# All expert weights resident on the chip; VectorE copies a tile's first half, TensorE streams the second from a register address

## The reference

```
p = softmax(LN(x) @ gate_w); pick the 2 best of E = 8 experts per token
h = gelu(LN(x) @ w1[e] + b1[e])        # w1[e]: 128 x 512
y = h @ w2[e] + b2[e]                  # w2[e]: 512 x 128
out = x + LN(x) ... + sum over the 2 experts of p_e * y_e
```

## Time and profile before

| | |
|---|---|
| profiled execution | 472.98 us; its span, first to last instruction, 471.3 us |
| granted TensorE clock, mean | 0.947 of 2.4 GHz |
| busy: TensorE, weight loads, VectorE, ScalarE, GpSimd | 397.6, 311.8, 280.9, 213.8, 137.6 us |
| DMA | 53.72 MB, mean 114 GB/s |
| weights by tile, `w1s` and `w2s` | 42 DMAs each, 256 KB, 3.5 us to landing |
| chain that ended last | PE 36%, issue 22%, DVE 18%, POOL 9%, DMA 6%, SyncE's queue 4% |

### The profile page before, as it was taken

One profiled execution on the slowest core, in us unless ns is written; L12 is line 12 of the kernel. 1 busy time (PEld: TensorE's weight loads), 2 busy tenths in 40 slices (PEclk: granted clock), 3 DMA queues, 4 the chain that ended last, 5 costly groups with the idle time before them and its releaser, 6 DMA issues.

```text
span 471.3 us, 8956 instructions
## 1 busy us (share of the span) xinstructions
PE 397.6 (84%) x2864; PEld 311.8 (66%) x2864; DVE 280.9 (60%) x905; ACT 213.8 (45%) x456; POOL 137.6 (29%) x139
## 2 busy tenths in 40 slices
PE   3547959989999999999999975979898898867963
PEld 2335747574488655885578634869798787866863
DVE  1388798799998689878987699323611011012322
ACT  1229376717636436322632351355543455534421
POOL 7743051431301250021642366010300000064343
PEclk9986979999999999999999995998979899999988
DMA  5999200000000000000400012424655778897542
GB/s 153 351 376 428 113 0 2 3 0 1 1 1 1 2 1 1 1 2 1 156 24 1 11 36 73 140 58 130 198 182 183 237 235 269 248 302 231 185 153 67
DMA packets 36117, 53.72 MB, mean 114 GB/s; under 512 B 5722, under 2 KB 20065, under 8 KB 34793
## 3 DMA queue, kind: packets, MB, share of 16 engines
q1 hardware_dynamic: 33512, 47.66, 30.1%
q0 software_dynamic: 2560, 5.52, 3.9%
HBM read 40.18 MB, written 12.98 MB: 113 GB/s over the span
## 4 chain that ended last, share of the span: by engine, by line
PE 36%; issue 22%; DVE 18%; POOL 9%; DMA 6%; SPq 4%; ACT 4%; POOLq 0%; DVEq 0%; ACTq 0%
POOL qkv L743 4%; PE bank L882 3%; PE bank L935 3%; DMA qkv<-experts_out,arena 3%; PE bank L948 3%; PE bank L964 3%; PE bank L987 2%; PE bank L920 2%; POOL dealt L729 2%; PE bank L980 2%; PE bank L972 2%; DVE h L1729 2%; PE bank L929 2%; SPq L567 2%; SPq L568 2%
## 5 line engine op out<-in xcount | busy, mean ns | idle before, releaser
L1275 ACT ACTIVATE arena<-bank,arena 128x128 f32<-128x128 f32 x168 | 47.9, 371 | 62.8 <-PE bank L1062 62.2
L743 POOL DMA_INDIRECT qkv<-experts_out,arena x28 | 26.5, 946 | 98.7 <-issue 80.2
L1070 PE MATMUL bank<-w2s,arena 128*128 128x128 f32 x336 | 48.0, 290 | 1.3 <-ACT arena L1275 1.3
L1070 PEld LDWEIGHTS bank<-w2s,arena 128*128 128x128 f32 x336 | 44.4, 205 | 2.3 <-ACT arena L1275 1.1
L729 POOL DMA_INDIRECT dealt<-xy,arena x28 | 32.5, 1161 | 29.2 <-DVE arena L1662 21.5
L1717 DVE COPY big<-bank 128x128 f32<-128x128 f32 x22 | 6.3, 290 | 46.6 <-PE bank L1070 46.6
L1062 PE MATMUL bank<-big,w1s 128*128 128x128 f32 x176 | 24.1, 281 | 10.2 <-DMA w1s<-in_ew 7.1
L1062 PEld LDWEIGHTS bank<-big,w1s 128*128 128x128 f32 x176 | 21.3, 191 | 12.5 <-issue 6.5
L1062 PE MATMUL bank<-arena,w1s 128*128 128x128 f32 x160 | 24.1, 299 | 5.9 <-DMA w1s<-in_ew 5.9
L935 PE MATMUL bank<-xT_f,wq 128*128 128x512 f32 x64 | 28.9, 597 | 0.0
L1062 PEld LDWEIGHTS bank<-arena,w1s 128*128 128x128 f32 x160 | 21.8, 211 | 7.3 <-issue 4.9
(11 more groups left out here) (266 smaller groups left out, 959.2 us busy)
## 6 DMA issues: line engine op xcount, KB each, us to landing
w1s<-in_ew SPq DMA_DIRECT2D x42, 256.0 KB, 3.5
w2s<-in_ew SPq DMA_DIRECT2D x42, 256.0 KB, 3.5
dealt<-lb SPq DMA_DIRECT2D x7, 1024.0 KB, 13.3
big<-in_tv SPq DMA_DIRECT2D x2, 2048.0 KB
big<-in_ew SPq DMA_DIRECT2D x16, 256.0 KB, 4.6
big<-dealt SPq DMA_DIRECT2D x22, 64.0 KB, 2.0
arena<-dealt SPq DMA_DIRECT2D x20, 64.0 KB, 1.8
experts_out<-arena SPq DMA_DIRECT2D x5, 256.0 KB, 4.1
```

The source lines that it names most:

```text
L743: pool.indirect_dma_start(yg[:, k, t, :], None, ys[g], bass.IndirectOffsetOnAxis(ap=posi[g][:, k, at:at + 1], axis=0)).then_inc(s_yg[b], 16)
L1070: last = pe.matmul(p[:, 0:D], hid[n % 2][:, c * P:(c + 1) * P], w2s[n % WAYS][:, c * D:(c + 1) * D], start=(c == 0), stop=(c == FC - 1))
L1275: last = act.activation(hid[n % 2][:, c * P:(c + 1) * P], of("K.up", n)[:, c * P:(c + 1) * P], ACT.Gelu, bias=eb1[:].rearrange("p e c -> p ...
```

## The change

All 8 experts' weights become resident in `big` (`rw1`, `rw2`, 4 MB, the whole buffer). V0 to V7 load them, at the head of SyncE's list. Section L is gone. Instead VectorE gets a phase K.0: a register load of `eid`, then a copy of 128x512 from `big` at a register address into `w1s` (still a ring of three). K.3 on TensorE gets a register load of `eid`, and its moving operand is read from `big` at a register address. K.1 is as before but waits for the copy. J reads `rw1`, `rw2` in place. What lay in `big` moves: tiles from 20 on into the buffers `u`, `fs`, `sq` of layer 0, J's hidden tiles into `ht`. All five lists are reordered.

```diff
     "K.dve2": ["y"],
+    "K.dve": ["w1"],
...
-        w1s = [sb("w1s%d" % i, [P, FF]) for i in range(3)]
-        w2s = [sb("w2s%d" % i, [P, FF]) for i in range(3)]
+        w1s = [sb("w1s%d" % i, [P, FF]) for i in range(WAYS)]
...
+        rw1 = big[:, 0:E * FF].rearrange("p (e f) -> p e f", e=E)
+        rw2 = big[:, E * FF:].rearrange("p (e f) -> p e f", e=E)
+        rest = [x[:].rearrange("p t c -> p (t c)")[:, k * T * D:(k + 1) * T * D].rearrange("p (t c) -> p t c", t=T)
+                for x in (u, fs, sq) for k in range(2)]
...
-            def section_L(n, ph):
-                g, j = OF_TILE[n]
-                wait(sp, "Z.dve.ei", g)
-                e = sp.value_load(eid[g][0:1, j:j + 1], min_val=0, max_val=E - 1)
-                wait(sp, "K.pe.up", n - WAYS)
-                sp.dma_start(w1s[n % WAYS][:], a["ew1"].rearrange("p e f -> p (e f)")[:, bass.ds(e * FF, FF)])\
-                  .then_inc(s_w1s[n % WAYS], 16)
-                wait(sp, "K.pe2.down", n - WAYS)
-                sp.dma_start(w2s[n % WAYS][:], a["ew2"].rearrange("p e f -> p (e f)")[:, bass.ds(e * FF, FF)])\
-                  .then_inc(s_w2s[n % WAYS], 16)
...
             def section_V(e, ph):
                 wait(sp, "H.pe.w2", B - 1)
-                wait(sp, "J.pe.up1", e - WAYS)
-                wait(sp, "J.pe2.down", e - WAYS)
-                for k, src in enumerate((a["ew1"], a["ew2"])):
-                    sp.dma_start(jw[e % WAYS][:, k, :], src[:, e, :]).then_inc(s_jw[e % WAYS], 16)
+                sp.dma_start(rw1[:, e, :], a["ew1"][:, e, :]).then_inc(s_ew[e], 16)
+                sp.dma_start(rw2[:, e, :], a["ew2"][:, e, :]).then_inc(s_ew[e], 16)
...
             def section_K(n, ph):                                  # TensorE
...
-                    pe.wait_ge(s_w1s[n % WAYS], 16 * (n // WAYS + 1))
+                    wait(pe, "K.dve.w1", n)
...
                 if ph == 3:
                     p = room(pe, "K.down", n)
-                    pe.wait_ge(s_w2s[n % WAYS], 16 * (n // WAYS + 1))
+                    wait(pe, "Z.dve.ei", g)
+                    for k in range(E if n == 0 else 0):
+                        pe.wait_ge(s_ew[k], 32)
+                    e = pe.value_load(eid[g][0:1, j:j + 1], min_val=0, max_val=E - 1)
                     wait(pe, "K.act.ht", n)
                     for c in range(FC):
                         last = pe.matmul(p[:, 0:D], hid[n % 2][:, c * P:(c + 1) * P],
-                                         w2s[n % WAYS][:, c * D:(c + 1) * D], start=(c == 0), stop=(c == FC - 1))
+                                         big[:, bass.ds(e * FF + (E * FF + c * D), D)], start=(c == 0), stop=(c == FC - 1))
...
             def section_K(n, ph):                                  # VectorE
                 g, j = OF_TILE[n]
+                if ph == 0:
+                    for k in range(E if n == 0 else 0):
+                        dve.wait_ge(s_ew[k], 32)
+                    wait(dve, "Z.dve.ei", g)
+                    e = dve.value_load(eid[g][0:1, j:j + 1], min_val=0, max_val=E - 1)
+                    wait(dve, "K.pe.up", n - WAYS)
+                    did(dve.tensor_copy(w1s[n % WAYS][:], big[:, bass.ds(e * FF, FF)]), "K.dve.w1", n)
```

More of the change, by code:

```diff
@@ L126 @@
     "sp": (
[4 rows of a table removed]
+        "V0.0 V1.0 V2.0 V3.0 V4.0 V5.0 V6.0 V7.0 X0.0 X1.0 X2.0 X3.0 X4.0 W0.0 W1.0 X5.0 W2.0 X6.0 X7.0 X8.0 X9.0 "
+        "W3.0 W4.0 X10.0 W5.0 W6.0 W7.0 W8.0 W9.0 W10.0 U0.0 U1.0 U2.0 U3.0"),
     "pool": (
[2 rows of a table removed]
[2 rows of a table added]
         "F3.3 I2.1 R1.3 R2.3 I3.1 R3.3 Y0.0 Y1.0 Y2.0 Y3.0"),
     "pe": (
[16 rows of a table removed]
-    "act": (
[12 rows of a table removed]
[16 rows of a table added]
+    "act": (
[12 rows of a table added]
     "dve": (
@@ L380, in lm_tower @@
         tv2 = big[:, E * FF:].rearrange("p (i f) -> p i f", i=E)
-        take = carve(big, 2 * E * FF)
-        xg0b = take([P, NT[0] - OWN, D])
-        xg1 = take([P, NT[1], D])
-        def tiles(g, j, m):
-            if g:
-                return xg1[:, j:j + m, :]
-            return xg0[:, j:j + m, :] if j < OWN else xg0b[:, j - OWN:j - OWN + m, :]
-        jw = [take([P, 2, FF]) for i in range(WAYS)]
-        hj = [take([P, FC, HALF * P]) for i in range(2)]
+        rw1 = big[:, 0:E * FF].rearrange("p (e f) -> p e f", e=E)
+        rw2 = big[:, E * FF:].rearrange("p (e f) -> p e f", e=E)
+        rest = [x[:].rearrange("p t c -> p (t c)")[:, k * T * D:(k + 1) * T * D].rearrange("p (t c) -> p t c", t=T)
+                for x in (u, fs, sq) for k in range(2)]
+        homes = dict(zip([(g, j) for g, j, m in BATCHES if g or j >= OWN], rest))
+        def tiles(g, j, m):
+            if g or j >= OWN:
+                return homes[g, j // T * T][:, j % T:j % T + m, :]
+            return xg0[:, j:j + m, :]
+        hj = [ht[:].rearrange("p c s -> p (c s)")[:, i * FC * HALF * P:(i + 1) * FC * HALF * P]
+              .rearrange("p (c s) -> p c s", c=FC) for i in range(2)]
         s1_i = few("s1_i", [P, 2, T])
@@ L512, in lm_tower @@
         s_ys = [ctx.enter_context(nc.semaphore("s_ys%d" % g)) for g in range(2)]
-        s_w2s = [ctx.enter_context(nc.semaphore("s_w2s%d" % i)) for i in range(WAYS)]
-        s_w1s = [ctx.enter_context(nc.semaphore("s_w1s%d" % i)) for i in range(WAYS)]
-        s_jw = [ctx.enter_context(nc.semaphore("s_jw%d" % i)) for i in range(WAYS)]
+        s_ew = [ctx.enter_context(nc.semaphore("s_ew%d" % e)) for e in range(E)]
         s_yg = [ctx.enter_context(nc.semaphore("s_yg%d" % b)) for b in range(B)]
@@ L601, in section_U @@
                              h[:, b * T:(b + 1) * T, :]).then_inc(s_out, 16)
-            each("sp", {"X": section_X, "L": section_L, "W": section_W, "V": section_V, "U": section_U})
+            each("sp", {"X": section_X, "W": section_W, "V": section_V, "U": section_U})
             sp.wait_ge(s_out, 16 * B)
@@ L1016, in section_J @@
             def section_J(e, ph):
-                w = jw[e % WAYS]
                 if ph == 0:
@@ L1021, in section_J @@
                         wait(pe, "I.act.xT", B - 1)
-                        pe.wait_ge(s_jw[e % WAYS], 32 * (e // WAYS + 1))
+                        pe.wait_ge(s_ew[e], 32)
                         for k in range(2):
                             c = 2 * n + k
-                            last = pe.matmul(p[:, k * HALF * P:(k + 1) * HALF * P], w[:, 0, c * P:(c + 1) * P],
+                            last = pe.matmul(p[:, k * HALF * P:(k + 1) * HALF * P], rw1[:, e, c * P:(c + 1) * P],
                                              xT_i[:, HALF * P:], start=True, stop=True)
@@ L1033, in section_J @@
                             last = pe.matmul(p[:, t * P:(t + 1) * P], hj[e % 2][:, c, t * P:(t + 1) * P],
-                                             w[:, 1, c * D:(c + 1) * D], start=(c == 0), stop=(c == FC - 1))
+                                             rw2[:, e, c * D:(c + 1) * D], start=(c == 0), stop=(c == FC - 1))
                     did(last, "J.pe2.down", e)
```

## The result

The changed kernel takes 449.84 us at the median of four runs (448.5 to 454.54), the kernel before 476.61 in the four beside it (475.28 to 479.73): ratio 0.945, 95% interval 0.936 to 0.953. The profiled execution took 449.65, its span 447.9 us, against 472.98 and 471.3. So of the 26.8 us between the medians the two traces can explain 23.4; the rest is that the profiled execution of before lay 3.6 under this median. The forecast was 459 in a range of 448 to 473: the direction and the mechanism hold, the gain was larger than forecast.

A forecast was written before the change was run, and what follows sets the result against it. Both TensorE's expert stage, delayed by SyncE's queue, and GpSimd's gathers bound the kernel. Span 389.0 + 4.25 + 58.4 - 1.5 + 1.5 + 0.6 = 452.3, 19.0 under 471.3; off the median 477.7 gives 459, range 448 to 473.

The forecast's parts named there:

- Bound by TensorE with `w1s` loads in its way: Expert stage: TensorE 92 of 104 us busy, its largest wait the `w1s` loads in SyncE's queue, 13.0 us in 12 waits.
- only the visible waits go: Rival on TensorE's stage: only the 13.0 us of visible waits vanish, the rest comes back as other waits; 465, chance 0.18.
- 76.0 us of pace, 8.5 of stalls, tile 30 at 389.0: TensorE from 304.5: 76.0 at its own pace, stalls 1.9 (Q2), 2.5 (layer norm), 4.1 rest; tile 30 ends 19.6 earlier.
- Register work on TensorE, 0.1 a tile: Register load before each tile's second half, covered by the first half's 0.89 us: 3.1 us in 31 tiles; bounds 0 and 0.97.
- The row of ScalarE: Nearest trace row for register work: two ScalarE tiles, a register load between, run 8 activations in 2.21 us without a gap.
- Copies: 42 VectorE copies 128x512, 0.43 us each, 18 us in all, taken as covered; bounds 0 and 0.43 a tile on TensorE's path.
- Collisions with GpSimd, 1.5 us: Nine VectorE copies among the gathers: five collisions of 0.33 us taken, 1.5 on the path, between 0 and 13.
- Gather chain, 59.0: GpSimd's four gather parts after tile 30: 58.4, less 1.5 for DMA sharing, plus 1.5 collisions, plus 0.6 for J7's sums.
- my 452.3: Forecast end of the profiled span, 452.3 against 471.3: tile 30 at 389.0, write and wait 4.25, then the gather chain.
- collisions (470): Rival at the gathers: nine copies cost the 1.43 of the worst row each, 13 in place of 1.5; 470, chance 0.06.
- exposed register work (475): Rival on TensorE: the up half does not cover the register work, 0.5 more a tile, +15.5; 475, chance 0.12.
- The slower one (498): Rival: TensorE's sequencer reads registers only with an empty array, 1.35 us a tile in place of 0.1, +39; 498, chance 0.07.

The follow-up runs named there:

- first pair: The changed kernel and the kernel before as first measured side by side, chip not on record: 449.84 us against 476.61, ratio 0.945.
- five-load trace: Changed kernel with four further register loads of the same value ahead of each down half on TensorE: 541.7 us, 1.120 against the kernel before.
- third chip: Chip of the third group of experiments, where the changed kernel was repeated unchanged: 460.8 us, 0.961 against the kernel before at 479.4.

## Why the prediction held, step by step

- **Bound by TensorE with `w1s` loads in its way**: right. Residency alone gives 0.951. The idle time that vanished (7.4 us) is less than the 13.0 of the earlier trace rows, which I read as waits of the stage, since half of them (6.6) lay behind tile 30, but the restarts and the clock behind them gave some 6 us more. The prediction named these as hidden in busy time and did not price them one by one; the sum from TensorE's own pace contained them. The rival "only the visible waits go" (465) fell by that.
- **76.0 us of pace, 8.5 of stalls, tile 30 at 389.0**: measured 78.1 busy (restarts are in it) and 5.1 idle, 387.7. The stalls were sized too high: Q2 waited 0.50 us for its inputs and not 1.9, the copy behind the last layer norm cost 0.8 and not 2.5.
- **Register work on TensorE, 0.1 a tile**: right as an upper figure, 0 to 3.1 us in all. The row of ScalarE was the right neighbour, and the upper bound of 0.97 a tile was ten times too high. What I gave as the reason, cover by the half in front, is one form of the sum above: 1.4 us of sequencer under 1.79 of array. The Trainium skill (TensorE: Matmul & The Clock Gate, Architectural detail) has a queue 64 deep, from which I had worked out no cost at all. The trace agrees for one load and not as a rule, for with five the pace is the sequencer's 4.0 us a tile, however deep the queue.
- **Copies**: 0.43 us as taken, and covered. Not foreseen: on VectorE the register load is exposed, so that two copies in a row stand 0.78 us apart, 0.35 of it idle (389.25 in the rows below). TensorE waits 3.49 us at 406.68 for a copy queued behind the sum Y0.1. In the first pair neither lengthens the chain of gathers.
- **Collisions with GpSimd, 1.5 us**: too high, and the earlier trace rows was read wrongly, as the rows below show. Seven copies fall among the gathers of the first pair, and one gather in 28 is longer, by 0.2 us. The Trainium skill (SBUF — State Buffer, SBUF: two separate sides) has such a DMA blocked until VectorE's instruction ends, which agrees with these rows. Its example, 620 ns that become 3100, is not of their size: the longest gather beside a copy takes 1.24 us.
- **Gather chain, 59.0**: 57.1. Parts take 15.7, 15.0, 15.5, 10.9 against 17.0, 15.8, 14.8, 10.9. The first is 1.3 us shorter, near the 1.5 put for the shared DMA engines; that this is the reason is not shown. Write and wait were kept at 4.25 and took 3.1.

Copies and gathers of the changed kernel in the first pair:

```profile
389.25 0.43 DVE L1710 COPY w1s<-big 128x512 f32 x1 [0.35 <-issue]
393.71 0.43 DVE L1710 COPY w1s<-big 128x512 f32 x1 [0.35 <-issue]
408.89 0.43 DVE L1710 COPY w1s<-big 128x512 f32 x1 [0.35 <-PE bank L1048]
```

```profile
393.32 0.94 POOL L730 DMA_INDIRECT qkv<-experts_out,arena  x1 [0.30 <-issue]
408.99 1.15 POOL L730 DMA_INDIRECT qkv<-experts_out,arena  x1 [0.30 <-issue]
```

The longer gather is the one that starts while a copy is running. The one at 393.32, in the middle of which a copy starts, takes 0.94 us like the others. The same holds for the gathers of all the traces: one is longer, by 0.09 to 0.3 us, when 0.22 to 0.38 us of a copy are left as it starts, and not when the copy starts later or has under 0.15 us left. So a copy costs a gather at most its own rest. In the earlier trace rows the TENSOR_SCALAR at 236.39 starts 0.56 us into the DMA of 235.83. What was running when that DMA began is a scan of VectorE, which ends at 236.35:

```profile
235.13 1.22 DVE L1532 TENSOR_TENSOR_SCAN lb<-la 128x512 f32<-128x512 f32 x1
```

The 2.39 us at 270.56, the worst row, are no collision with one instruction either: VectorE's instructions run without a gap from before its start until 1.62 us into it. The copies of the change have 0.35 us between them and never add up so.

Together: 1.3 (tile 30) + 1.1 (write) + 1.9 (chain) = 4.3 us under my 452.3, which is the measured span of 447.9 but for rounding. The terms that were mis-sized are the new stalls and the collisions, all of them priced as if they fell on the path. In tile 30's time two errors cancel in part: stalls 3.4 us too high, pace 2.1 too low. The rest of the difference to 459, some 4.6 us, is the step from the trace to the median: the median of before stood 4.8 above its profiled execution, I took the same for the new kernel, and there it is 0.2. That is the spread of the runs and not something that the mechanism gives.

The rivals: collisions (470) and exposed register work (475) are refuted by the rows above. The slower one (498) is refuted for one load. (Its 1.35 us a tile is summed wrongly: 0.77 + 4 x 0.1 + 0.28 is 1.45, which gives 501.) It was nearer than it looked: with three loads the sequencer would take some 1.4 + 2 x 0.64 = 2.7 us a tile, an estimate from the five-load trace. That is 0.9 over TensorE's 1.79, and the loss begins at 0.65 to 0.8.

## What to carry to other kernels

Where one engine's queue issues inputs, weights and results in turn, count issues per tile, not bytes: here 237 GB/s beside the stage cost 0.8 to 2.9 us, while taking the issues away gave 17 (101.2 to 84.4). On TensorE an address from a register was free here as long as all the sequencer's work of a tile (0.64 us a load, 0.1 an address) stayed under the tile's compute. On VectorE it was not: the same load left 0.35 us idle before a copy. And a term of the sum that stands on an engine with slack goes in at nothing, with its price kept for the range.

## What the runs showed of the hardware

- On the three chips of the experiments TensorE's results reach ScalarE late beside rows of indirect DMAs: the latest gelu of each trace with rows of eight comes 2 to 8 us after its half's last matmul, and 25 us behind 24 in a row; in the first pair of traces never more than 1.1. The time of the same kernel differs by 2.4% between the first pair and the third chip (449.8 and 460.8 us), and its ratio to the kernel before by 1.6 points; the late results are part of that.
- Two register loads in a row on TensorE's sequencer are 0.64 us apart, though the load itself takes 0.30.
- An indirect DMA that starts while 0.22 to 0.38 us of a 128x512 fp32 copy are left takes 0.09 to 0.3 us longer (0.94 us otherwise). A copy that starts during the DMA cost none of them anything.
